# A recommendation tower on one core: ids loaded ahead of tables, and each pair's last gathered unit handled in two halves of its batches

## The chip, the cores and the metric

The kernel runs on one NeuronCore of a Trainium2 chip. The metric is the device time of one execution in microseconds (us), as a median over runs; lower is better.

## The reference

For each of 2048 batches, 26 rows of 128 numbers are looked up, one in each of 26 tables. The 27 vectors of a batch (the dense one and the 26 looked up) are multiplied with each other in pairs, and the 351 products, with the dense vector before and behind them, go through three dense layers.

```python
e = jnp.stack([tbl_0[ids[:, 0]], tbl_1[ids[:, 1]], ..., tbl_25[ids[:, 25]]], axis=1)
sd = jnp.einsum('bfd,bd->bf', e, r_dense_features)
ss = jnp.einsum('bfd,bgd->bfg', e, e)
pairs = ss[:, iu, ju]
z = jnp.concatenate([r_dense_features, sd, pairs], axis=1)
h = jnp.concatenate([z, r_dense_features], axis=1)
h = jnp.maximum(h @ W_top1 + b_top1, 0.0)
h = jnp.maximum(h @ W_top2 + b_top2, 0.0)
y = h @ W_top3
```

Everything is 32-bit floating point. The tables have 1000, 1250, 12500 or 125000 rows.

## The kernel before

The 2048 batches are cut into 8 chunks of 256, and two chunks make a pair: there are 4 pairs. All five engines have a program of their own, written out by hand, with semaphores between them. TensorE (PE) and ScalarE (ACT) both walk through the same list of steps for each pair, in the strings FIRST, SECOND, THIRD, LAST and TAIL; a step is a letter and a number, and each engine does its own part of the letters that concern it. The letters that matter here are these.

- `l`: one of the 12 (in later pairs 11) tables of 1000 rows is looked up on TensorE. The table lies in SBUF as two fp32r parts, `table_hi` and `table_lo`, and is multiplied with a one-hot matrix that VectorE (DVE) makes from the ids: 8 rows of the table for each of 125 partitions, in four parts, so 16 matmuls of 512 columns for a pair (L593). `c` is the copy of the result into `feat` by ScalarE (L434).
- `i` and `j`: ScalarE shifts the ids of one lookup for the one-hot comparison (L417). `s`: ScalarE makes `table_hi` of a table (L412). VectorE makes `table_lo` (L496), and then two comparisons for each of the four parts (L505). It does this for the tables in order, so that `make_part` of lookup 6 stands right behind its first `split_lo`, and waits for `ids_shifted`.
- `r` and `q`: a unit of gathered rows is turned. GpSimd (POOL) gathers the rows of the other 14 tables, two tables to a unit, with one indirect DMA for each table and each 128 batches: 4 a unit (L395), into a ring of 6 units. TensorE transposes the 4 blocks of 128x128 into one of two banks of `tr_ps` (L569), and ScalarE copies the bank into `feat` (L426). `q14` is the last unit of a pair, and belongs to its second chunk.
- `d` and `e`: the products of a chunk, in 8 steps of 32 matmuls (L611), `e` for the first chunk of a pair and `d` for the second. Step v covers batches 32v to 32v+31 of the chunk, so `d0` to `d3` read the first 128 batches and `d4` to `d7` the second. Each step's output is copied half by ScalarE (L441) and half by VectorE (L514).
- `k`, `o`, `m`: the dense layers of a chunk (L632, L641), for which the products go out to HBM and come back (L306, L319) through SyncE (SP).
- `f` and `g`: ScalarE copies the dense features of a chunk into `feat` (L421).

SyncE issues the loads in program order from L325 on: the first six tables with their ids, two more tables, the dense features of chunk 0, the row numbers (`idx`) of the gathers of pair 1, and then for u = 8 to 11 table u and ids u-2, and at last ids 10 and 11. A table is 1000x128 floats, 500 KB; the ids of one lookup are 128x512 of 16 bits, 128 KB; the dense features of a chunk are 128 KB, the `idx` of a pair 30 KB.

The wait at the head of the second chunk's products covers all the units of the pair:

```python
if v == 0:
    pe.wait_ge(transposed_out, unit_no(n // 2, UNITS if n % 2 else ALONE + has_odd(n // 2)))
```

Of the kernel before, what the change touches and what calls it, by code (L numbers as in the profile page):

```python
# [10 lines left out]
P = 128  # L11
# [9 lines left out]
CH = 256  # L21
# [47 lines left out]
SECOND = ("l0 l1 q12 l2 q13 l3 q14 d0 d1 d2 d3 d4 d5 d6 c2 d7 c3 r0 o0 c0 o1 c1 o2 r1 o3 r2 o4 i6 "  # L69
          "l4 c4 r3 i7 l5 c5 r4 i8 l6 c6 r5 l7 c7 i9 l8 c8 r6 i10 f l9 c9 r7 l10 c10 r8 "  # L70
          "j0 m0 g m1 e0 e1 e2 e3 r9 e4 e5 e6 e7 r10 m2 j1 m3 j2 r11 m4 j3 r12 j4 j5")
THIRD = ("l0 l1 q13 o0 q14 o1 d0 d1 d2 d3 d4 d5 d6 c0 d7 c1 r0 o2 o3 r1 o4 r2 "
         "l2 c2 r3 i6 l3 c3 i7 l4 c4 r4 i8 l5 c5 r5 l6 c6 i9 r6 l7 c7 i10 f l8 c8 r7 l9 c9 r8 l10 c10 r9 "
         "j0 m0 g m1 e0 e1 r10 e2 e3 e4 e5 e6 e7 r11 m2 j1 r12 m3 j2 j3 m4 r13 j4 j5")
LAST = ("l0 l1 q14 o0 o1 r0 d0 d1 d2 d3 d4 d5 d6 c0 d7 c1 r1 o2 o3 r2 o4 r3 "
        "l2 c2 l3 c3 r4 i6 l4 c4 r5 i7 l5 c5 i8 r6 l6 c6 i9 r7 f l7 c7 i10 l8 c8 r8 l9 c9 r9 g l10 c10 r10 "
        "m0 m1 e0 e1 e2 e3 r11 e4 e5 e6 e7 r12")
TAIL = "k2 q13 k3 q14 d0 d1 d2 d3 d4 d5 d6 d7 k4 o0 o1 o2 o3 o4 m0 m1 m2 m3 m4"
# [40 lines left out]
def dlrm_tower(nc, dense_t, dense_f, idx, ids_t, tables, w1, b1, w2, b2, w3, y):  # L119
# [6 lines left out]
    with ctx:  # L126
# [70 lines left out]
        onehot_read = sem("onehot_read")  # L197
        transposed = sem("transposed")
# [64 lines left out]
        def _(sp):  # L263
# [66 lines left out]
            for u in range(IDSLOTS, RAWS):  # L330
                load_table(u)
            load_dense(0)
            load_idx(1)
            for u in range(RAWS, NO + 1):
                load_table(u)
                load_ids(u - RAWS + IDSLOTS)
            for u in range(NO + 1 - RAWS + IDSLOTS, NO + 1):
                load_ids(u)
# [39 lines left out]
        @block.gpsimd  # L378
        def _(pool):
            nc.gpsimd.iota(row_i[:], [[1, 1]], base=0, channel_multiplier=-RPP)  # L380
            nc.gpsimd.iota(diag, [[1, P]], base=0, channel_multiplier=-1).then_inc(iotas_made, 1)

            for j, u in itertools.product(range(NPAIR), range(UNITS)):
                if u == ALONE and not has_odd(j):
                    continue
                i = unit_no(j, u)
                if u == 0:
                    pool.wait_ge(idx_loaded[j % 2], DMA * (j // 2 + 1))
                if i >= RING:
                    pool.wait_ge(transposed, i - RING + 1)  # L390
                for k in range(2):
                    f = ODD if u == ALONE else UNIT[u % (ALONE + 1)][k]
                    for t in range(TILES):
                        x = (2 * u + k) * TILES + t
                        nc.gpsimd.indirect_dma_start(  # L395
                            rows[:, i % RING, k, t, :], None, tables[f],
                            bass.IndirectOffsetOnAxis(ap=idx_sb[:, j % 2, x:x + 1], axis=0),
                        ).then_inc(rows_loaded[i % RING], DMA)
# [3 lines left out]
        def _(act):  # L402
# [20 lines left out]
            def transposed_to_feat(j, u):  # L423
                i = unit_no(j, u)
                act.wait_ge(transposed, i + 1)
                nc.scalar.activation(unit_view(u), tr_ps[:, i % 2], ACT.Copy).then_inc(transposed_out, 1)  # L426

# [27 lines left out]
            for j in range(NPAIR + 1):  # L455
                n = 2 * j
                for kind, x in steps(ORDER[j]):
# [12 lines left out]
                    if kind == "q":  # L470
                        transposed_to_feat(j - 1, x)
                    if kind == "f":
# [86 lines left out]
        def _(pe):  # L559
            def transposes(j, u):  # L560
                i = unit_no(j, u)
                pe.wait_ge(rows_loaded[i % RING], DMA * TILES * 2 * (i // RING + 1))
                if i == 0:
                    pe.wait_ge(ident_made, 1)
                if i >= 2:
                    pe.wait_ge(transposed_out, i - 1)
                for k in range(2):
                    for t in range(TILES):
                        last = nc.tensor.transpose(tr_ps[:, i % 2, k, t * P:(t + 1) * P], rows[:, i % RING, k, t, :],  # L569
                                                   ident[:])  # L570
# [28 lines left out]
            def dot_products(n, v):  # L599
                if v == 0:  # L600
                    pe.wait_ge(transposed_out, unit_no(n // 2, UNITS if n % 2 else ALONE + has_odd(n // 2)))
# [48 lines left out]
            for j in range(NPAIR + 1):  # L650
                n = 2 * j
                for kind, x in steps(ORDER[j]):
# [4 lines left out]
                    if kind == "q":  # L657
                        transposes(j - 1, x)
                    if kind == "d":
# [54 lines left out]
```

## Time and profile before

| | |
|---|---|
| median of 3 runs | 357.22 us (357.12 to 358.61) |
| the profiled execution, its own time | 358.96 us |
| its span, first to last instruction | 357.1 us |
| PE busy | 342.4 us, 96% |
| PE weight loads busy | 290.9 us, 81% |
| DVE busy | 207.0 us, 58% |
| ACT busy | 205.9 us, 58% |
| POOL busy | 239.0 us, 67% |
| mean granted clock of TensorE | 0.99 |

The span is measured between the first and the last instruction; the execution's own time has 1.9 us more around it. Busy time of PE counts matmuls from issue to their modelled end, so it says that PE nearly always has something in flight, and not that it runs at its peak. "PEclk" is the granted clock of TensorE as a share of full speed. A row of a timeline has start, duration, engine, line, operation, output and inputs with shapes, count, and in brackets the idle time of the engine just before it and what ended it.

### The profile page before, as it was taken

To read this page: it belongs to the slowest core of one execution; us is meant where nothing else is said; L and a number is where in the kernel's file an instruction comes from. 1 tells how busy PE (TensorE), PEld (TensorE's weight loads), DVE (VectorE), ACT (ScalarE), POOL (GpSimd) and SP (SyncE) were. 2 spreads that over 40 slices of the span, in tenths; PEclk is the share of its full clock that TensorE was granted. 3 is DMA by queue.
4 is the path that set the end of the run, shared out by engine and by line. 5 is a ranking of instruction groups with operands and counts; after the bars stand their busy time and mean duration, and the time that the engine had idled before them with its cause. 6 is when DMAs were issued, how large, how long until landed. Compare 5 with 4: busy or idle time off the path is not lost.

```text
span 357.1 us, 8384 instructions
## 1 busy us (share of the span) xinstructions
PE 342.4 (96%) x3412; PEld 290.9 (81%) x3412; DVE 207.0 (58%) x522; ACT 205.9 (58%) x268; POOL 239.0 (67%) x242
## 2 busy tenths in 40 slices
PE   8897899999899999999999999999999999998996
PEld 7575687788778888888988888898988888888885
DVE  4895899677504884716428784527327777235111
ACT  4674698762583657663565555772672675575111
POOL 5777777777777777777777777777777777700000
PEclk9999699999999999999999999999999999999999
DMA  7999829545246215263255224254246221223410
GB/s 192 237 232 229 216 54 285 146 104 148 56 116 197 54 45 156 56 147 107 59 131 168 63 61 143 54 120 137 54 101 185 73 62 50 53 58 98 97 40 2
DMA packets 46488, 40.94 MB, mean 115 GB/s; under 512 B 29059, under 2 KB 40443, under 8 KB 46451
## 3 DMA queue, kind: packets, MB, share of 16 engines
q1 hardware_dynamic: 38755, 24.81, 26.8%
q0 software_dynamic: 7552, 15.48, 17.2%
q8 instruction: 27, 0.44, 0.5%
q10 hardware_dynamic: 144, 0.13, 0.1%
q14 instruction: 10, 0.08, 0.1%
HBM read 34.64 MB, written 5.76 MB: 113 GB/s over the span
## 4 chain that ended last, share of the span: by engine, by line
PE 87%; DMA 7%; ACT 2%; DVE 2%; issue 1%; SPq 1%; ACTq 0%; DVEq 0%
PE oh_ps L593 39%; PE mlp_ps L632 16%; PE dot_ps L611 16%; PE mlp_ps L641 8%; PE tr_ps L569 7%; DMA ids_bc<-ids_t_dram 6%; PE mlp_ps L593 2%; DMA dots<-tbl_dram 2%; ACT feat L426 1%; DVE onehot L505 1%; ACT feat L434 0%; ACT ids_bc L417 0%; ACT table_hi L412 0%; DVE table_lo L496 0%; SPq L286 0%
## 5 line engine op out<-in xcount | busy, mean ns | idle before, releaser
L395 POOL DMA_INDIRECT rows<-tbl_dram,idx_sb x236 | 238.5, 1010 | 73.6 <-issue 70.7
L505 DVE TENSOR_SCALAR onehot<-ids_bc 125x512 fp32r<-125x512 int16 x360 | 142.9, 443 | 37.0 <-PE oh_ps L593 16.6
L593 PE MATMUL oh_ps<-onehot,table_hi 125*128 125x512 f32 x344 | 112.1, 408 | 5.4 <-DVE onehot L505 5.4
L593 PE MATMUL oh_ps<-onehot,table_lo 125*128 125x512 f32 x344 | 107.8, 395 | 0.0
L426 ACT ACTIVATE feat<-tr_ps 128x512 f32<-128x512 f32 x59 | 72.8, 1234 | 31.4 <-PE tr_ps L569 30.8
L434 ACT ACTIVATE feat<-oh_ps 128x512 f32<-128x512 f32 x43 | 52.4, 1219 | 55.2 <-PE oh_ps L593 54.5
L593 PEld LDWEIGHTS oh_ps<-onehot,table_hi 125*128 125x128 f32 x344 | 62.0, 192 | 20.4 <-issue 9.9
L593 PEld LDWEIGHTS oh_ps<-onehot,table_lo 125*128 125x128 f32 x344 | 65.5, 190 | 14.5
L611 PE MATMUL dot_ps<-feat 128*54 128x52 f32 x2048 | 57.9, 214 | 3.9 <-ACT feat L426 2.5
L611 PEld LDWEIGHTS dot_ps<-feat 128*54 128x54 f32 x2048 | 54.6, 130 | 8.6 <-issue 3.5
L514 DVE COPY dots<-dot_ps 54x416 f32<-54x416 f32 x56 | 33.3, 594 | 36.4 <-PE dot_ps L611 28.3
L632 PE MATMUL mlp_ps<-zt,w_sb 117*128 117x256 f32 x192 | 44.1, 380 | 0.8 <-ACT feat L434 0.8
L521 DVE TENSOR_TENSOR h<-mlp_ps,b_sb 128x256 f32<-128x256 f32 x16 | 6.8, 424 | 59.9 <-PE mlp_ps L641 59.9
L632 PEld LDWEIGHTS mlp_ps<-zt,w_sb 117*128 117x128 f32 x192 | 35.3, 190 | 5.3 <-issue 1.0
L441 ACT ACTIVATE dots<-dot_ps 54x416 f32<-54x416 f32 x56 | 28.9, 518 | 17.3 <-PE dot_ps L611 13.7
L569 PE MATMUL tr_ps<-ident,rows 128*128 128x128 f32 x236 | 36.0, 275 | 0.0
L417 ACT ACTIVATE ids_bc<-ids_bc,row_f 128x512 int16<-128x512 int16 x45 | 31.0, 702 | 6.5 <-DMA ids_bc<-ids_t_dram 6.5
L569 PEld LDWEIGHTS tr_ps<-ident,rows 128*128 128x128 f32 x236 | 28.5, 140 | 6.6
L448 ACT ACTIVATE h<-mlp_ps,b_sb 128x256 f32<-128x256 f32 x32 | 15.1, 471 | 25.9 <-PE mlp_ps L632 25.7
L641 PE MATMUL mlp_ps<-w_sb,h 128*128 128x256 f32 x128 | 29.0, 380 | 0.0
L641 PEld LDWEIGHTS mlp_ps<-w_sb,h 128*128 128x128 f32 x128 | 24.0, 190 | 3.1
L632 PE MATMUL mlp_ps<-feat,w_sb 117*128 117x256 f32 (+1 forms) x64 | 14.2, 379 | 0.0
(32 smaller groups left out, 98.3 us busy)
## 6 DMA issues: line engine op xcount, KB each, us to landing
ids_bc<-ids_t_dram SPq DMA_DIRECT2D x44, 128.0 KB, 3.4
dots_scratch<-dots SPq DMA_DIRECT2D x28, 175.5 KB
rows<-tbl_dram,idx_sb POOLq DMA_INDIRECT x236
dots<-tbl_dram SPq DMA_DIRECT2D x5, 480.0 KB
w_sb<-tbl_dram SPq DMA_DIRECT2D x3, 480.0 KB
zt<-dots_scratch SPq DMA_DIRECT2D x12, 117.0 KB
dense_sb<-dense_f_dram SPq DMA_DIRECT2D x8, 128.0 KB, 3.1
zt<-tbl_dram SPq DMA_DIRECT2D x2, 480.0 KB
```

The lines of the kernel that those rows point to most:

```text
L395: nc.gpsimd.indirect_dma_start(rows[:, i % RING, k, t, :], None, tables[f], bass.IndirectOffsetOnAxis(ap=idx_sb[:, j % 2, x:x + 1], axis=0 ...
L417: nc.scalar.activation(ids, ids, ACT.Identity, bias=row_f[:, 0:1]).then_inc(ids_shifted, 1)
L426: nc.scalar.activation(unit_view(u), tr_ps[:, i % 2], ACT.Copy).then_inc(transposed_out, 1)
L434: nc.scalar.activation(both, lookup_out(m).rearrange("p (c b) -> p c b", c=2), ACT.Copy).then_inc(looked_up_out, 1)
L441: nc.scalar.activation(*dot_copy(n, v, 0), ACT.Copy).then_inc(dots_out_act, 1)
L505: last = nc.vector.tensor_scalar(onehot_part(m, part)[:, c, :], ids_bc[0:TP, m % IDSLOTS, :], float(part * PROWS + c), None, ALU.is_equal)
L514: nc.vector.tensor_copy(*dot_copy(n, v, 1)).then_inc(dots_out_dve, 1)
L569: last = nc.tensor.transpose(tr_ps[:, i % 2, k, t * P:(t + 1) * P], rows[:, i % RING, k, t, :], ident[:])
L593: last = nc.tensor.matmul(lookup_out(m), table[0:TP, u, row * D:(row + 1) * D], onehot_part(m, part)[:, c, :], start=(table is table_hi an ...
L611: last = nc.tensor.matmul(dot_ps[dot_rows(t), v % 2, gi * PACK * NJ:(gi + 1) * PACK * NJ], batches.rearrange("p q f -> p (q f)"), batches[ ...
L632: last = nc.tensor.matmul(mlp_ps[:, x % 2, 0:CH], w1_sb[0:m, c, x * P:(x + 1) * P], z_of(n)[0:m, c, :], start=(c == 0), stop=(c == ZC))
L641: last = nc.tensor.matmul(mlp_ps[:, t, 0:N2], h1[:, c, t * P:(t + 1) * P], w2_sb[:, c, :], start=(c == 0), stop=(c == N1 // P - 1))
```

## The change

Two things are changed. SyncE issues the ids of lookup u-2 ahead of table u for u = 8 to 11, and issues the dense features of chunk 0 and the `idx` of pair 1 after all of these loads instead of before them. And the last unit of each pair is handled by halves of its batches: GpSimd gathers both tables' rows of the first 128 batches and then both of the second, each half with a semaphore of its own; step `q14` transposes and copies the first half only (2 transposes, a copy of 128x256), into columns 0 to 127 of one bank, and a new step `p` does the second, in the other bank. The products `d0` wait for the first half, and `d4` for the second.

```diff
--- before.py
+++ after.py
@@ -66,16 +66,16 @@
...
-SECOND = ("l0 l1 q12 l2 q13 l3 q14 d0 d1 d2 d3 d4 d5 d6 c2 d7 c3 r0 o0 c0 o1 c1 o2 r1 o3 r2 o4 i6 "
+SECOND = ("l0 l1 q12 l2 q13 l3 q14 d0 p d1 d2 d3 d4 d5 d6 c2 d7 c3 r0 o0 c0 o1 c1 o2 r1 o3 r2 o4 i6 "
...
-TAIL = "k2 q13 k3 q14 d0 d1 d2 d3 d4 d5 d6 d7 k4 o0 o1 o2 o3 o4 m0 m1 m2 m3 m4"
+TAIL = "k2 q13 k3 q14 d0 p d1 d2 d3 d4 d5 d6 d7 k4 o0 o1 o2 o3 o4 m0 m1 m2 m3 m4"
...
@@ -329,13 +333,13 @@
                 load_table(u)
             for u in range(IDSLOTS, RAWS):
                 load_table(u)
+            for u in range(RAWS, NO + 1):
+                load_ids(u - RAWS + IDSLOTS)
+                load_table(u)
+            for u in range(NO + 1 - RAWS + IDSLOTS, NO + 1):
+                load_ids(u)
             load_dense(0)
             load_idx(1)
-            for u in range(RAWS, NO + 1):
-                load_table(u)
-                load_ids(u - RAWS + IDSLOTS)
-            for u in range(NO + 1 - RAWS + IDSLOTS, NO + 1):
-                load_ids(u)
             load_dense(1)
             for u in range(3):
                 load_ids(looked(1) + u)
@@ -388,6 +392,14 @@
                     pool.wait_ge(idx_loaded[j % 2], DMA * (j // 2 + 1))
                 if i >= RING:
                     pool.wait_ge(transposed, i - RING + 1)
+                if u == UNITS - 1:
+                    for t, k in itertools.product(range(TILES), range(2)):
+                        x = (2 * u + k) * TILES + t
+                        nc.gpsimd.indirect_dma_start(
+                            rows[:, i % RING, k, t, :], None, tables[UNIT[ALONE - 1][k]],
+                            bass.IndirectOffsetOnAxis(ap=idx_sb[:, j % 2, x:x + 1], axis=0),
+                        ).then_inc(half_rows[t], DMA)
+                    continue
                 for k in range(2):
                     f = ODD if u == ALONE else UNIT[u % (ALONE + 1)][k]
                     for t in range(TILES):
@@ -422,8 +434,19 @@
 
             def transposed_to_feat(j, u):
                 i = unit_no(j, u)
+                if u == UNITS - 1:
+                    act.wait_ge(first_half_turned, j + 1)
+                    nc.scalar.activation(unit_view(u)[:, :, 0:P], tr_ps[:, i % 2, :, 0:P], ACT.Copy
+                                         ).then_inc(first_half_out, 1)
+                    return
                 act.wait_ge(transposed, i + 1)
                 nc.scalar.activation(unit_view(u), tr_ps[:, i % 2], ACT.Copy).then_inc(transposed_out, 1)
+
+            def second_half_to_feat(j):
+                i = unit_no(j, UNITS - 1)
+                act.wait_ge(transposed, i + 1)
+                nc.scalar.activation(unit_view(UNITS - 1)[:, :, P:CH], tr_ps[:, (i + 1) % 2, :, P:CH], ACT.Copy
+                                     ).then_inc(transposed_out, 1)
 
             def looked_up_to_feat(j, u):
                 m = looked(j) + u
...
@@ -557,17 +582,40 @@
 
         @block.tensor
         def _(pe):
+            def turn(j, u, bank, k, t):
+                i = unit_no(j, u)
+                return nc.tensor.transpose(tr_ps[:, bank, k, t * P:(t + 1) * P], rows[:, i % RING, k, t, :], ident[:])
+
             def transposes(j, u):
                 i = unit_no(j, u)
-                pe.wait_ge(rows_loaded[i % RING], DMA * TILES * 2 * (i // RING + 1))
+                if u == UNITS - 1:
+                    pe.wait_ge(half_rows[0], 2 * DMA * (j + 1))
+                else:
+
+                    ahead = sum(unit_no(h, UNITS - 1) % RING == i % RING for h in range(j))
+                    pe.wait_ge(rows_loaded[i % RING], DMA * TILES * 2 * (i // RING + 1 - ahead))
                 if i == 0:
                     pe.wait_ge(ident_made, 1)
                 if i >= 2:
-                    pe.wait_ge(transposed_out, i - 1)
+
+                    pe.wait_ge(transposed_out, i - (u > 0))
+                if u == UNITS - 1:
+                    for k in range(2):
+                        last = turn(j, u, i % 2, k, 0)
+                    last.then_inc(first_half_turned, 1)
+                    return
                 for k in range(2):
                     for t in range(TILES):
-                        last = nc.tensor.transpose(tr_ps[:, i % 2, k, t * P:(t + 1) * P], rows[:, i % RING, k, t, :],
-                                                   ident[:])
+                        last = turn(j, u, i % 2, k, t)
+                last.then_inc(transposed, 1)
+
+            def second_half(j):
+
+                i = unit_no(j, UNITS - 1)
+                pe.wait_ge(half_rows[1], 2 * DMA * (j + 1))
+                pe.wait_ge(transposed_out, i)
+                for k in range(2):
+                    last = turn(j, UNITS - 1, (i + 1) % 2, k, 1)
                 last.then_inc(transposed, 1)
 
             def lookup(j, u):
@@ -597,8 +645,14 @@
                     last.then_inc(onehot_read, 1)
 
             def dot_products(n, v):
+                if n % 2 and v == 0:
+                    pe.wait_ge(transposed_out, unit_no(n // 2, UNITS - 1))
+                    pe.wait_ge(first_half_out, n // 2 + 1)
+                if n % 2 and v == GUNITS // TILES:
+                    pe.wait_ge(transposed_out, unit_no(n // 2, UNITS))
+                if n % 2 == 0 and v == 0:
+                    pe.wait_ge(transposed_out, unit_no(n // 2, ALONE + has_odd(n // 2)))
                 if v == 0:
-                    pe.wait_ge(transposed_out, unit_no(n // 2, UNITS if n % 2 else ALONE + has_odd(n // 2)))
                     pe.wait_ge(looked_up_out, looked(n // 2 + 1))
                     pe.wait_ge(dense_out, n + 1)
                 if n or v >= 2:
...
```

Left out are the same new step `p` in THIRD (`q14 p o1 d0`) and LAST (`q14 p o0 o1 r0 d0`), the new semaphores, and the two lines by which TensorE and ScalarE do `p` for the pair before.

The loads that SyncE issues, from the last of the first eight tables on, in the kernel before (`dots`, `zt` and `w2_sb` hold raw tables here; `tbl_19` is table 8 in the text):

```order
L297 DMA w2_sb<-tbl_16_dram 5x1024
L278 DMA dense_sb<-dense_f_dram 128x256
L267 DMA idx_sb<-idx_dram 128x60
L296 DMA dots<-tbl_19_dram 120x1024 [waits lo_made]
L297 DMA dots<-tbl_19_dram 5x1024
L273 DMA ids_bc<-ids_t_dram 128x512 [waits onehot_made]
L296 DMA dots<-tbl_21_dram 120x1024 [waits lo_made]
```

The same place of the changed kernel:

```order
L301 DMA w2_sb<-tbl_16_dram 5x1024
L277 DMA ids_bc<-ids_t_dram 128x512 [waits onehot_made]
L300 DMA dots<-tbl_19_dram 120x1024 [waits lo_made]
L301 DMA dots<-tbl_19_dram 5x1024
L277 DMA ids_bc<-ids_t_dram 128x512 [waits onehot_made]
L300 DMA dots<-tbl_21_dram 120x1024 [waits lo_made]
```

The ids of lookup 6 stand right behind table 7: dense features, `idx` and table 8 are no longer ahead of them. The two small loads follow at the end of the row of loads:

```order
L300 DMA zt<-tbl_25_dram 120x1024 [waits lo_made]
L301 DMA zt<-tbl_25_dram 5x1024
L277 DMA ids_bc<-ids_t_dram 128x512 [waits onehot_made] x2
L282 DMA dense_sb<-dense_f_dram 128x256
L271 DMA idx_sb<-idx_dram 128x60
```

On TensorE, the last pair's last unit ahead of the last chunk's products (TAIL), in the kernel before:

```order
L632 MATMUL mlp_ps<-zt,w1_sb 128x256 x3
L569 MATMUL tr_ps<-ident,rows 128x128 [waits transposed_out,rows_loaded4]
L569 MATMUL tr_ps<-ident,rows 128x128 x3
L611 MATMUL dot_ps<-feat 54x52 [waits dots_out_act,dense_out,dots_out_dve,looked_up_out,transposed_out]
L611 MATMUL dot_ps<-feat 54x52 x15
L611 MATMUL dot_ps<-feat 54x52 [waits dots_out_dve,dots_out_act]
```

And in the changed kernel:

```order
L686 MATMUL mlp_ps<-zt,w1_sb 128x256 x3
L587 MATMUL tr_ps<-ident,rows 128x128 [waits transposed_out,half_rows0]
L587 MATMUL tr_ps<-ident,rows 128x128
L665 MATMUL dot_ps<-feat 54x52 [waits dense_out,dots_out_act,looked_up_out,dots_out_dve,first_half_out,transposed_out]
L665 MATMUL dot_ps<-feat 54x52 x15
L587 MATMUL tr_ps<-ident,rows 128x128 [waits transposed_out,half_rows1]
L587 MATMUL tr_ps<-ident,rows 128x128
L665 MATMUL dot_ps<-feat 54x52 [waits dots_out_dve,dots_out_act]
```

Two of the four transposes are moved behind `d0`, with a wait of their own for the second half of the rows.

## Rows read from the trace of the kernel before

**Rows 1.** The page: busy time of each engine.
```profile
PE 342.4 (96%) x3412; PEld 290.9 (81%) x3412; DVE 207.0 (58%) x522; ACT 205.9 (58%) x268; POOL 239.0 (67%) x242
```

**Rows 2.** Waits of PE: engine, line, waited for, us in total, times, longest.
```profile
PE oh_ps L593 <- DVE onehot L505: 5.4, 2, 4.1
PE dot_ps L611 <- ACT feat L426: 2.5, 2, 1.3
```

**Rows 3.** The chain that ended last, at the sixth ids: start, us, what.
```profile
14.79 20.59 DMA ids_bc<-ids_t_dram
...
35.41 0.73 ACT ids_bc L417
```

**Rows 4.** Timeline around PE's longest wait: DVE twice, then DVE and PE.
```profile
27.14 0.41 DVE L496 TENSOR_TENSOR table_lo<-w_sb,table_hi 125x256 fp32r<-125x256 f32 x1
...
31.27 0.41 DVE L496 TENSOR_TENSOR table_lo<-w_sb,table_hi 125x256 fp32r<-125x256 f32 x1
...
36.16 0.90 DVE L505 TENSOR_SCALAR onehot<-ids_bc 125x512 fp32r<-125x512 int16 x2 [4.48 <-ACT ids_bc L417]
...
37.20 1.19 PE L593 MATMUL oh_ps<-onehot,table_hi 125*128 125x512 f32 x2 [4.06 <-DVE onehot L505]
```

**Rows 5.** Windows: stretch, length, busy of PE, PEld, DVE, ACT, POOL, PEclk, DMA, GB/s.
```profile
33.14:37.20 4.06, 0.00 (x1) 0.03 (x1) 1.04 (x3) 1.79 (x3) 3.15 (x4) 0.87 1.01 234
37.20:43.43 6.23, 6.22 (x16) 4.88 (x17) 5.09 (x16) 3.69 (x4) 4.83 (x5) 0.53 0.92 226
43.98:47.50 3.52, 3.52 (x18) 2.93 (x17) 3.09 (x9) 3.52 (x4) 2.85 (x3) 1.00 0.27 75
```

**Rows 6.** Tile ids_bc on SP's queue: ids 5, 8 and 11 with landings.
```profile
L273 SPq DMA_DIRECT2D ids_bc<-ids_t_dram x1: 351/351/351, 8.5 to 8.5; - x1
DMA to landing us min/median/max: 12.3/12.3/12.3
...
L273 SPq DMA_DIRECT2D ids_bc<-ids_t_dram x1: 699/699/699, 24.2 to 24.2; - x1
DMA to landing us min/median/max: 18.4/18.4/18.4
...
L273 SPq DMA_DIRECT2D ids_bc<-ids_t_dram x1: 328/328/328, 31.4 to 31.4; - x1
DMA to landing us min/median/max: 14.5/14.5/14.5
```

**Rows 7.** Timeline, DVE: the one-hots of lookup 11's last part and the next six.
```profile
62.08 2.96 DVE L505 TENSOR_SCALAR onehot<-ids_bc 125x512 fp32r<-125x512 int16 x8
```

**Rows 8.** Timeline, ACT: the dense copy `f` and the table step `s10`.
```profile
51.45 0.83 ACT L421 ACTIVATE feat<-dense_sb 128x256 f32<-128x256 f32 x1
...
53.04 1.18 ACT L412 ACTIVATE table_hi<-dots 125x1024 fp32r<-125x1024 f32 x1
```

**Rows 9.** Timeline, PE: the products of chunk 1 after `q14` (SECOND).
```profile
91.42 7.46 PE L611 MATMUL dot_ps<-feat 128*54 128x52 f32 x256 [1.27 <-ACT feat L426]
```

**Rows 10.** Timeline of the tail: a dense copy, two gathers, `q14` and its copy.
```profile
302.68 0.77 ACT L421 ACTIVATE feat<-dense_sb 128x256 f32<-128x256 f32 x1
...
309.82 0.95 POOL L395 DMA_INDIRECT rows<-tbl_dram,idx_sb  x1 [0.30 <-issue]
...
312.32 0.94 POOL L395 DMA_INDIRECT rows<-tbl_dram,idx_sb  x1 [0.30 <-issue]
...
320.59 0.60 PE L569 MATMUL tr_ps<-ident,rows 128*128 128x128 f32 x4
...
321.23 1.18 ACT L426 ACTIVATE feat<-tr_ps 128x512 f32<-128x512 f32 x1
```

**Rows 11.** The chain: four transposes between products.
```profile
312.14 0.59 PE tr_ps L569 x4
```

**Rows 12.** Tile ids_bc on SP's queue, 52 to 54 us: landing of lone loads.
```profile
DMA to landing us min/median/max: 2.3/2.4/3.8
```

More of the change, by code:

```diff
@@ L68 @@
          "e4 e5 g j2 e6 e7 r11 j3 j4 j5")
-SECOND = ("l0 l1 q12 l2 q13 l3 q14 d0 d1 d2 d3 d4 d5 d6 c2 d7 c3 r0 o0 c0 o1 c1 o2 r1 o3 r2 o4 i6 "
+SECOND = ("l0 l1 q12 l2 q13 l3 q14 d0 p d1 d2 d3 d4 d5 d6 c2 d7 c3 r0 o0 c0 o1 c1 o2 r1 o3 r2 o4 i6 "
           "l4 c4 r3 i7 l5 c5 r4 i8 l6 c6 r5 l7 c7 i9 l8 c8 r6 i10 f l9 c9 r7 l10 c10 r8 "
           "j0 m0 g m1 e0 e1 e2 e3 r9 e4 e5 e6 e7 r10 m2 j1 m3 j2 r11 m4 j3 r12 j4 j5")
-THIRD = ("l0 l1 q13 o0 q14 o1 d0 d1 d2 d3 d4 d5 d6 c0 d7 c1 r0 o2 o3 r1 o4 r2 "
+THIRD = ("l0 l1 q13 o0 q14 p o1 d0 d1 d2 d3 d4 d5 d6 c0 d7 c1 r0 o2 o3 r1 o4 r2 "
          "l2 c2 r3 i6 l3 c3 i7 l4 c4 r4 i8 l5 c5 r5 l6 c6 i9 r6 l7 c7 i10 f l8 c8 r7 l9 c9 r8 l10 c10 r9 "
          "j0 m0 g m1 e0 e1 r10 e2 e3 e4 e5 e6 e7 r11 m2 j1 r12 m3 j2 j3 m4 r13 j4 j5")
-LAST = ("l0 l1 q14 o0 o1 r0 d0 d1 d2 d3 d4 d5 d6 c0 d7 c1 r1 o2 o3 r2 o4 r3 "
+LAST = ("l0 l1 q14 p o0 o1 r0 d0 d1 d2 d3 d4 d5 d6 c0 d7 c1 r1 o2 o3 r2 o4 r3 "
         "l2 c2 l3 c3 r4 i6 l4 c4 r5 i7 l5 c5 i8 r6 l6 c6 i9 r7 f l7 c7 i10 l8 c8 r8 l9 c9 r9 g l10 c10 r10 "
         "m0 m1 e0 e1 e2 e3 r11 e4 e5 e6 e7 r12")
-TAIL = "k2 q13 k3 q14 d0 d1 d2 d3 d4 d5 d6 d7 k4 o0 o1 o2 o3 o4 m0 m1 m2 m3 m4"
+TAIL = "k2 q13 k3 q14 d0 p d1 d2 d3 d4 d5 d6 d7 k4 o0 o1 o2 o3 o4 m0 m1 m2 m3 m4"
 ORDER = [FIRST, SECOND, THIRD, LAST, TAIL]
@@ L197, in dlrm_tower @@
         onehot_read = sem("onehot_read")
+        half_rows = [sem(f"half_rows{t}") for t in range(TILES)]
+        first_half_turned = sem("first_half_turned")
+        first_half_out = sem("first_half_out")
         transposed = sem("transposed")
@@ L471, in _ @@
                         transposed_to_feat(j - 1, x)
+                    if kind == "p":
+                        second_half_to_feat(j - 1)
                     if kind == "f":
@@ L658, in _ @@
                         transposes(j - 1, x)
+                    if kind == "p":
+                        second_half(j - 1)
                     if kind == "d":
```

## The prediction

> **What bounds the kernel now.** I read the page first: PE is busy for 96% of the span and the other engines for 58 to 67% [rows 1], so time is lost only where PE stands still or runs slowly. The waits of PE name both places: 5.4 us for one-hots, of which one wait is 4.1 us, and 2.5 us, in two waits, for ScalarE's copy of a unit ahead of the products [rows 2]. A third loss is not a wait at all: the windows show TensorE's clock.
>
> The long wait, followed back. The chain says that the ids of lookup 6 were issued at 14.79 and landed 20.59 us later, at 35.38, that ScalarE then shifted them [rows 3], and that VectorE, idle for 4.48 us, began the one-hots at 36.16; PE, idle for 4.06 us, started lookup 6 at 37.20 [rows 4]. The table part that VectorE makes just before these one-hots was there at 31.27 + 0.41 = 31.68 [rows 4], so it was the ids alone that were missing. They were late because of what SyncE had put ahead of them: in issue order dense features, `idx` and table 8, and those behind tables 5 to 7.
>
> The clock. In the stretch in which PE idles, the granted clock falls (0.87 on average), and in the whole of lookup 6 behind it, it is 0.53, so near the lower level of 1.2 GHz; in lookup 7 it is 1.00 again [rows 5]. Lookup 6 with its 16 matmuls takes 6.23 us, lookup 7 takes 3.52 in the stretch shown [rows 5].
>
> **The ids moved ahead.** From the landing of ids 5 (8.5 + 12.3 = 20.8) [rows 6] to that of ids 6 (35.4) the queue moved tables 5 to 8, dense features, `idx` and ids 6, 2000 + 128 + 30 + 128 = 2286 KB in 14.6 us, 157 KB a us. From ids 6 to ids 8 (24.2 + 18.4 = 42.6) [rows 6] it moved two tables and two ids, 1256 KB in 7.2 us, 174 KB a us. The change takes table 8, dense features and `idx`, 658 KB, out from ahead of ids 6: 4.2 us by the first rate, 3.8 by the second. I take 4.2, since it is the rate of that very stretch; ids 6 then land at 31.2, and VectorE starts 0.78 later as before, at 31.98, 0.3 us after its table part is ready. PE ends the transposes ahead of lookup 6 at 33.14 and needs the one-hots about 1.04 us after VectorE begins (36.16 to 37.20), so at 33.02: no wait.
>
> From there VectorE sets the pace. Its first table parts of lookups 5 and 6 stand 31.27 - 27.14 = 4.13 us apart [rows 4]. From the first one-hots of lookup 6 to the last part of lookup 11 are 5.75 lookups, 23.7 us. Before, they took 62.08 - 36.16 = 25.9 [rows 4, 7]: 2.2 us more, lost while PE at half clock held the one-hot buffers. Now the last part starts at 31.98 + 23.7 = 55.7 instead of 62.08, **6.35 us earlier** (4.2 of wait and 2.15 of slow clock). Lookups 7, 8 and 9 need their ids at 36.1, 40.2 and 44.4. Counting the bytes ahead of each, ids 7 now stand where ids 6 stood, less dense features and `idx`, plus ids 7: 35.2 + 0.8 for the shift, 36.0. Ids 8 come one table and one load of ids later (628 KB, 4.0 us), shifted at 40.0, ids 9 at 44.0. All are just in time, none with more than 0.4 us in hand.
>
> **The 2.15 us hang on what made the clock fall.** The rows show one fall, behind PE's longest wait: 0.13 x 4.06 + 0.47 x 6.23 = 3.5 us of missing clock [rows 5] is 1% of the span, all that its mean of 0.99 lacks, so PE's shorter waits (1.3 us and less [rows 2]) left it alone. If the clock fell for the idle time, no idle time means no fall, and the result is my sum, 351.4; if it fell for another cause, 2.15 us of the gain are gone, 353.6. The Trainium skill (TensorE: Matmul & The Clock Gate, Part 1: The HAM clock gate) says that the throttled state is the default and that activity releases it. By that rule the sum stays whole, and the trace agrees: 0.53 behind the idle stretch, 1.00 after one lookup.
>
> **The two loads moved behind.** The dense features of chunk 0 now come last. The bytes in the queue are the same in all, so they land about when ids 11 did, 31.4 + 14.5 = 45.9 [rows 6]. ScalarE copies them at 51.45 before and goes on to table 10's high part at 53.04 to 54.22 [rows 8]. Shifted by 6.35, the copy is wanted at 45.1 and the high part is done at 47.87, where VectorE wants it at 31.6 + 4 x 4.13 = 48.1. So ScalarE waits 0.8 to 1.0 us, 0.2 of it is slack, and **0.7 us** passes through VectorE to PE. It would be nothing if the loads drain faster, and 1.2 if the small load lands later still. `idx` of pair 1 is wanted by GpSimd only after 56 gathers of pair 0 at its pitch of 1.25 us or more (309.82 to 312.32 are two) [rows 10], so after 70 us: no cost. No load other than these three kinds changes place on SyncE.
>
> **The unit in halves.** Nothing is added to GpSimd's 236 gathers, which are only reordered. At the first boundary (SECOND) PE waits 1.27 us for the copy [rows 9]. Two transposes less ahead of the copy are 0.3 us (half of 0.60), and a copy of 128x256 takes 0.77 where 128x512 takes 1.18 [rows 10]: `d0` starts 0.7 earlier. Step `p` then costs PE two transposes between products; four cost 0.59 [rows 11], so 0.3, and I add 0.1 for the second switch. Net -0.3. ScalarE's second copy of 0.77 lies between its copies for `d0` and `d1`, where PE is not waiting for it: two banks are free before `d2`. In TAIL the copy starts at 321.23, after PE's transposes were done, because ScalarE is busy with a relu until then, so only 0.4 of copy is saved, and `p` costs 0.4: nothing. In THIRD and LAST the copy was hidden before by a layer step; there `p` costs 0.1 each for its wait and switch. Bounds of this part: -1.2 (two boundaries at 0.7, with transposes for nothing) to +0.9 (four times 0.4 less 0.7). Sum **-0.1**.
>
> **Sum.** -6.35 + 0.7 - 0.1 = **-5.8 us**. The profiled execution took 358.96 with a span of 357.1, so it would take 353.2 with a span of 351.3; it stood 1.7 above the median, and from the median, 357.22, I forecast 351.4.
>
> Does the gain live to the end? PE has work queued everywhere behind, and what could hold it is the gathers, since GpSimd never waits for PE and so doesn't move. Its last gather starts at 312.32 and ends at 313.26; `q14` comes at 320.59 [rows 10]. Lone loads land 2.3 to 3.8 us after issue [rows 12], so I let the rows land by 315.7 at best, by 317.1 at worst. With 5.8 us less, `q14` comes at 314.8 and needs only the first half, whose second gather starts at 309.82 and which lands by 314.6 at worst. `p` comes behind relu, copy and `d0`, at about 317.2. It is ready. Whole, the unit would have made PE wait 0.9 us or more, so here the halves guard what the ids win, and that is their use in the tail.
>
> **Rivals.**
> - *The wait moves to the next ids.* The queue stays full until 43 us, and ids 7 and 8 have 0.1 us in hand. If the queue is slower by a tenth, PE stands still for 1 to 2 us in pieces, and perhaps at a lower clock: 352.6 to 354.4. For it: the small margins. Against it: both rates come from this stretch. 0.14.
> - *The clock falls all the same*: 353.6, as above. 0.07.
> - *Issue order does not decide landing*, so the first part does nothing; with the halves alone, 357.1. The Trainium skill (DMA: Bandwidth & Descriptors, Queues, rings and completion order) says that descriptors are consumed in ring order, but that a later one may finish its write first. The landings of ids 6, 8 and 11 (35.4, 42.6, 45.9) follow the order and the bytes. 0.05.
> - *The last half of rows is late*: a gather that takes 4.8 us to land makes PE wait 1 us in `p`: 352.4. 0.05.
> - *Slower.* The dense copy `f` stands in ScalarE's order ahead of lookup 8's copy and of table 10, and ScalarE cannot pass it. From a landing of the dense features at 51.1 (45.1 + 0.2 + 5.8) on, the change costs more than it brings; with PE idle that long the clock would fall again, another 2.2 us, so it decides from about 49. At 52.5 the result is 361. For it: the loads are now last in the queue, behind two loads of ids that wait for one-hots. Against it: those waits are over at 31.4, the issue of ids 11 [rows 6]. 0.04.
>
> **Numbers.** The forecast has the rest, 0.65. A measurement of this kernel can tell about 0.5%, 1.8 us, from no change, so faster is below 355.4. The low end takes the full 6.35 with no wait for dense features and 0.9 at the boundaries, 350.0; the high end holds the cases of moved wait, kept slow clock and late half, 354.4. Left out are the third and fifth rival and the edges. Faster 0.90: all but those two. Same 0.06, slower 0.04.
>
> **What would show it.** In the new profile ids 6 land near 31 and PE goes from lookup 5 to 6 with under 1 us between; PEclk stays at 1.00 from 30 to 50 us; ScalarE's copy of dense features waits for a DMA at about 45 us; the products of chunk 0 begin near 60 instead of 65.5; PE's wait ahead of chunk 1's products is about 0.6 instead of 1.27; the last `p` waits for nothing and the last gather still starts near 312. The prediction is wrong if PEclk falls again, if ids 7 or 8 hold PE, or if PE waits in `p`.

## The result, and the profile after

The changed kernel takes **353.26 us** in the median of four runs (352.86 to 353.53), the kernel before took 357.59 beside it (357.12 to 358.61). The ratio is 0.9874, 95% interval 0.9849 to 0.99: faster, by 1.3%. The profiled execution took 353.4 with a span of 351.6, where before's had 358.96 and 357.1. One thing has to be known of the experiments: in two of their three sets every kernel, the one before included, took 466 to 488 us at a mean granted clock near 0.9, and the ratios, which are taken from the shorter executions of each kernel alone, can lie above 1 there while the medians of all lie below, so they decide little.

The page of the changed kernel, against [rows 1]:

```profile
PE 340.6 (97%) x3412; PEld 288.8 (82%) x3412; DVE 206.8 (59%) x522; ACT 205.7 (58%) x272; POOL 239.0 (68%) x242
...
PEclk9999999999999999999999999999999999999999
```

The first line is busy time by engine, the second TensorE's granted clock in 40 equal slices of the span, in tenths (9 is 90% or more). The waits of PE in the changed kernel, against [rows 2] (engine, tile and line, waited for: us in total, times, longest):

```profile
PE dot_ps L665 <- issue: 3.0, 4, 1.0
...
PE tr_ps L587 <- DMA rows<-tbl_dram,idx_sb: 1.3, 1, 1.3
...
PE oh_ps L641 <- DVE onehot L530: 0.8, 1, 0.8
```

Of 5.4 us for one-hots 0.8 is left, that of the first lookup. ScalarE's copy of a unit is no longer what the profile names at the end of a wait ahead of products; the gaps that are left there it calls "issue", which is time for which it shows no releaser. A new line has come in: 1.3 us for gathered rows, ahead of transposes.

The timeline of the changed kernel at the old long wait, ScalarE's rows first, then PE's, against [rows 3, 4]:

```profile
29.96 0.70 ACT L429 ACTIVATE ids_bc<-ids_bc,row_f 128x512 int16<-128x512 int16 x1
...
34.09 0.71 ACT L429 ACTIVATE ids_bc<-ids_bc,row_f 128x512 int16<-128x512 int16 x1
```
```profile
31.92 0.60 PE L587 MATMUL tr_ps<-ident,rows 128*128 128x128 f32 x4
32.28 0.70 PE L641 MATMUL oh_ps<-onehot,table_hi 125*128 125x512 f32 x2
...
37.48 0.66 PE L587 MATMUL tr_ps<-ident,rows 128*128 128x128 f32 x4 [1.28 <-DMA rows<-tbl_dram,idx_sb]
```

ScalarE shifts ids 6 at 29.96 (35.41 before) and ids 7 at 34.09 without waiting for either, and PE goes from the transposes into lookup 6 with no gap. The ids were issued at 11.5 and landed 18.4 us later, at 29.9. PE now waits at 37.48 instead, for rows.

The windows of 30 to 50 us (length, busy of PE, PEld, DVE, ACT, POOL, PEclk, DMA share, GB/s), of the changed kernel and then of the kernel before:

```profile
30.00:50.00 20.00, 18.62 (x89) 14.55 (x88) 18.95 (x55) 17.48 (x20) 15.43 (x16) 1.00 0.76 191
```
```profile
30.00:50.00 20.00, 15.94 (x64) 12.72 (x63) 13.90 (x40) 12.06 (x14) 15.43 (x16) 0.83 0.73 176
```

The clock no longer falls, and PE gets 89 matmuls done in this stretch instead of 64. GpSimd's column is the same in both: 16 gathers, since it waits for nobody here.

The chain that ended last, in the changed kernel, a little later:

```profile
33.28 1.04 POOL rows L407
34.32 0.31 issue
34.62 7.22 DMA rows<-tbl_dram,idx_sb
41.85 0.04 issue
41.89 0.66 PE tr_ps L587 x4
```

These rows took 7.22 us from the gather to the landing, where the page's median over all 236 gathers is 3.2. They came just in time for PE, the ones before them 1.3 us late.

Two of the four boundaries with a unit in halves, those at which PE had waited for the copy (SECOND and TAIL), in the changed kernel, against [rows 9, 10]:

```profile
83.80 0.38 PE L587 MATMUL tr_ps<-ident,rows 128*128 128x128 f32 x2
85.00 1.01 PE L665 MATMUL dot_ps<-feat 128*54 128x52 f32 x32 [0.81 <-issue]
85.93 0.44 PE L587 MATMUL tr_ps<-ident,rows 128*128 128x128 f32 x2
86.30 6.68 PE L665 MATMUL dot_ps<-feat 128*54 128x52 f32 x224
...
314.73 0.38 PE L587 MATMUL tr_ps<-ident,rows 128*128 128x128 f32 x2
316.07 1.01 PE L665 MATMUL dot_ps<-feat 128*54 128x52 f32 x32 [0.96 <-issue]
317.01 0.44 PE L587 MATMUL tr_ps<-ident,rows 128*128 128x128 f32 x2
317.38 3.00 PE L665 MATMUL dot_ps<-feat 128*54 128x52 f32 x104
320.77 3.40 PE L665 MATMUL dot_ps<-feat 128*54 128x52 f32 x120 [0.39 <-issue]
```

`q14`, `d0` and `p` stand as the change puts them, and `p` waits for nothing in either place. Read against the kernel before, PE is 5.74 us ahead at the first products (65.54 to 59.80), 6.42 at the products of chunk 1 (91.42 to 85.00), 5.86 at `q14` of the tail (320.59 to 314.73) and 5.47 at the last layer steps behind the products (329.57 to 324.10).

### The profile page after: what moved, and what is told of

Its sections match the earlier page's. It is cut to its first block, busy times and chain, and to the rows that moved or that the text cites. A ratio compares the mean times of both kernels' runs of the same rounds, so it can differ in the third digit from the quotient of the medians.

```text
span 351.6 us, 8396 instructions
## 1 busy us (share of the span) xinstructions
PE 340.6 (97%) x3412; PEld 288.8 (82%) x3412; DVE 206.8 (59%) x522; ACT 205.7 (58%) x272; POOL 239.0 (68%) x242
## 4 chain that ended last, share of the span: by engine, by line
PE 85%; POOL 7%; issue 3%; DMA 3%; ACT 1%; DVE 0%; ACTq 0%; DVEq 0%
PE oh_ps L641 36%; PE dot_ps L665 16%; PE mlp_ps L686 16%; PE mlp_ps L695 8%; PE tr_ps L587 7%; POOL rows L407 7%; PE mlp_ps L641 2%; DMA rows<-tbl_dram,idx_sb 2%; DMA idx_sb<-idx_dram 1%; ACT feat L443 0%; ACT feat L457 0%; DVE h L549 0%; ACT ids_bc L429 0%; DVE h L546 0%; ACT dots L464 0%
## 5 line engine op out<-in xcount | busy, mean ns | idle before, releaser
L641 PE MATMUL oh_ps<-onehot,table_hi 125*128 125x512 f32 x344 | 110.7, 403 | 0.8 <-DVE onehot L530 0.8
L641 PE MATMUL oh_ps<-onehot,table_lo 125*128 125x512 f32 x344 | 106.5, 391 | 0.0
L443 ACT ACTIVATE feat<-tr_ps 128x512 f32<-128x512 f32 x55 | 68.2, 1241 | 23.1 <-PE tr_ps L587 22.5
L641 PEld LDWEIGHTS oh_ps<-onehot,table_lo 125*128 125x128 f32 x344 | 64.6, 188 | 14.1
L641 PEld LDWEIGHTS oh_ps<-onehot,table_hi 125*128 125x128 f32 x344 | 60.8, 189 | 15.4 <-issue 6.0
```

The costliest lines, as they stand in the source:

```text
L641: last = nc.tensor.matmul(lookup_out(m), table[0:TP, u, row * D:(row + 1) * D], onehot_part(m, part)[:, c, :], start=(table is table_hi an ...
```

## The experiments

The theory was that the load order brings nearly all of the gain, as a wait and a slow clock that are both gone, and that the halves bring next to nothing by themselves and guard the gain in the tail. The rivals: the halves bring a good part of it; the clock's fall has another cause than idle time; the late rows cost what the ids win.

**A first set, of the parts.** Four kernels ran side by side. The kernel before, unchanged:

> The kernel before, unchanged. The changed kernel is 5.5 us shorter in the profiled spans, but 4.3 us in the medians. Theory: how long the clock stays at half level after the long wait differs from one execution to the next, so spans lie between about 355 and 357.1 and go with the mean clock (0.990 at 357.1, up to 0.995 at 355). Rival: the 1.2 us are time outside the span; then spans are 357 every time and the clock 0.990.

The load order alone (its edit stands with the second set):

> Only the order of SyncE's loads is changed; the last unit stays whole. Theory (the load order brings nearly all): span 351.6, within 0.5 us of the changed kernel; the products after q14 begin 5.7 us earlier at both exposed boundaries, and in the tail PE waits 0.3 us for the last rows (last gather issued at 312.3, landing 2.7 us). Rival (the halves carry part of it): PE waits over 1 us for the last rows, span 352.6 or more.

The halves alone:

> Only the last unit of each pair is done in halves; the loads are as before. Theory: what the earlier start of d0 saves (0.7 and 0.6 us at two boundaries) is given back by step p between products (0.4 to 0.9 each): span 357.0 to 357.6, no difference. Rival (the halves gain at the exposed boundaries, as forecast for SECOND): 356.5 or less.

And the change with the two small loads kept in front of ids 6:

```diff
+            load_dense(0)
+            load_idx(1)
             for u in range(RAWS, NO + 1):
                 load_ids(u - RAWS + IDSLOTS)
                 load_table(u)
             for u in range(NO + 1 - RAWS + IDSLOTS, NO + 1):
                 load_ids(u)
-            load_dense(0)
-            load_idx(1)
```

> The changed kernel, with dense features and idx ahead of ids 6 as before; only the ids stay ahead of the tables. Ids 6 then land 0.9 us later, near 30.9. Theory (behind the ids it is the landing of gathered rows that holds PE, at 37.5 us, whatever the one-hots do): span within 0.3 us of 351.6. Rival (VectorE's pace from ids 6 on sets the stage, as in my prediction): 0.7 us longer, 352.3.

The kernel before took 481.88 beside these (470.15 to 488.43, 23 runs). In the order above the medians were 478.25, 478.97, 478.49 and 479.52, the ratios 0.9992 (0.9878 to 1.0107), 0.999 (0.9906 to 1.0074), 1.0144 (1.0052 to 1.0236) and 1.0141 (1.0052 to 1.0231). The waits of PE in the unchanged kernel of this set say why that settles nothing:

```profile
PE dot_ps L611 <- issue: 33.3, 55, 1.2
PE oh_ps L593 <- DVE onehot L505: 19.9, 14, 4.1
PE oh_ps L593 <- issue: 18.6, 11, 4.6
```

These three rows hold 72 us of waits, spread over the whole span, and one-hots alone 20 us where [rows 2] have 5.4. A kernel with such gaps on every engine has other ends of waits than ours. Nor do the two ratios of 1.014 say that halves cost anything: they stand beside medians that are lower than the 481.88 of the kernel before.

**A second set, at the usual speed.** The kernel before took 356.97 (354.75 to 359.43, 25 runs). Against this median the changed kernel's 353.26 would be 0.9896, so its gain is better told as 1.0 to 1.3%: the four executions beside it had a median of 357.59.

The load order alone, on the kernel before:

```diff
-            load_dense(0)
-            load_idx(1)
             for u in range(RAWS, NO + 1):
-                load_table(u)
                 load_ids(u - RAWS + IDSLOTS)
+                load_table(u)
             for u in range(NO + 1 - RAWS + IDSLOTS, NO + 1):
                 load_ids(u)
+            load_dense(0)
+            load_idx(1)
```

> Only the order of SyncE's loads is changed; the last unit stays whole. Theory (the load order brings nearly all): span 351.6, within 0.5 us of the changed kernel; the products after q14 begin 5.7 us earlier at both exposed boundaries, and in the tail PE waits about 0.3 us for the last rows (last gather issued at 312.3, landing 2.7 us). Rival (the halves carry part of it): PE waits over 1 us for the last rows, span 352.6 or more.

Measured: 357.08 (355.26 to 358.25, ten runs), ratio 0.9998, interval 0.9965 to 1.0031. **The load order alone brings nothing that can be measured.** Its profile shows that it works where it should and loses the gain at the end. The timeline of PE in the tail:

```profile
311.04 0.66 PE L569 MATMUL tr_ps<-ident,rows 128*128 128x128 f32 x4
...
313.26 0.60 PE L569 MATMUL tr_ps<-ident,rows 128*128 128x128 f32 x4
313.70 1.90 PE L632 MATMUL mlp_ps<-zt,w_sb 117*128 117x256 f32 x8
317.14 0.66 PE L569 MATMUL tr_ps<-ident,rows 128*128 128x128 f32 x4 [1.55 <-DMA rows<-tbl_dram,idx_sb]
319.07 9.70 PE L611 MATMUL dot_ps<-feat 128*54 128x52 f32 x256 [1.27 <-ACT feat L426]
```

The chain at its last gather:

```profile
312.17 0.95 POOL rows L395
313.11 0.30 issue
313.42 3.68 DMA rows<-tbl_dram,idx_sb
```

And the windows there, of this kernel (the columns are those of the windows above):

```profile
310.00:315.00 5.00, 5.00 (x68) 4.52 (x63) 1.19 (x2) 3.75 (x5) 3.45 (x4) 1.00 0.38 89
315.00:320.00 5.00, 2.18 (x27) 1.54 (x27) 0.00 (x0) 1.74 (x3) 0.00 (x0) 0.81 0.62 146
320.00:325.00 5.00, 5.00 (x114) 5.00 (x112) 1.78 (x3) 1.53 (x3) 0.00 (x0) 0.51 0.25 75
325.00:330.00 5.00, 5.00 (x142) 4.65 (x139) 2.97 (x5) 2.56 (x5) 0.00 (x0) 1.00 0.02 7
```

PE comes to its first products at 60.47, 5.07 us ahead of before, and is still 5.16 ahead at `q13` (318.42 to 313.26). Then it reaches the last unit before its rows do: the chain has the last gather at 313.42 and 3.68 us to the landing. It waits 1.55 us, transposes for 0.67 us, waits 1.27 us for the whole unit's copy, and in the second of those waits the clock falls to the lower level (1.00 up to 317.80, 0.62 on average from there to 319.07, 0.50 behind it): the last 256 products take 9.70 us where they took 7.18 at 322.46 in the kernel before. By the steps behind them (329.57 to 328.70) 0.87 of the 5.16 us is left. In this profile the fall is not at the ids any more (PEclk is 1.00 from 30 to 50 us), it is at the end.

The size of that first wait has scatter in it. The last gather started at 313.42 here and at 312.32 in the kernel before. From there the same 3.68 us would have left PE a wait of about 0.4 us (an estimate: 316.0 less 315.6, where PE stopped). But two kernels with halves had a last gather nearly as late, at 313.08 (the halves alone, below) and 313.34 (units later, below), and PE waited for no rows in their tails, with `q14` at 315.11 and 314.80. In the profiles, then, the halves do guard the tail.

The halves alone, that is the change with the load order of the kernel before:

> Only the last unit of each pair is done in halves; the loads are as before. Theory: what the earlier start of d0 saves (0.7 and 0.6 us at two boundaries) is given back by step p between products (0.4 to 0.9 each): span 357.0 to 357.6 if the clock falls for as long as before, no difference. Rival (the halves gain at the exposed boundaries, as forecast for SECOND): 356.5 or less.

Measured: 355.72 (353.65 to 361.1, ten runs), ratio 0.9961, interval 0.9918 to 1.0003: a gain of 1.3 us at the edge of what can be told. Its profiled execution had a span of 351.8, as short as the changed kernel's, although its ids are loaded in the old order. Rows of that execution, ScalarE and PE at lookup 6:

```profile
32.08 0.72 ACT L429 ACTIVATE ids_bc<-ids_bc,row_f 128x512 int16<-128x512 int16 x1 [1.79 <-DMA ids_bc<-ids_t_dram]
```
```profile
33.78 0.70 PE L641 MATMUL oh_ps<-onehot,table_hi 125*128 125x512 f32 x2 [1.03 <-DVE onehot L530]
```

Here ScalarE, which waited for ids 6, took them up at 32.08 where it was 35.41 in [rows 3], 3.3 us earlier with the same loads in the same order, PE waited 1.03 us instead of 4.06, and the clock stayed at 1.00. The windows of 20 to 30 us, of the kernel before and then of this one, show where the 3.3 us come from:

```profile
20.00:30.00 10.00, 10.00 (x52) 8.07 (x51) 10.00 (x30) 8.88 (x10) 7.87 (x8) 1.00 1.01 234
```
```profile
20.00:30.00 10.00, 10.00 (x51) 8.11 (x50) 10.00 (x30) 9.23 (x10) 7.87 (x8) 1.00 1.00 258
```

With the DMA engines full in both (shares 1.01 and 1.00), they moved 234 GB/s in one execution and 258 in the other. Why is not shown. So **the loss that the change removes has no fixed size**. The other runs say the same: the 25 executions of the kernel before have spans from 352.9 to 357.6, eight at a mean clock of 1.00 or 0.999 (352.9 to 354.3), the others at 0.99 to 0.995 (353.2 to 357.6). Where the clock did not fall, the load order alone has little left to win: three of its executions have a clock of 1.00, with spans of 352.9 to 353.4. The changed kernel's four are at 351.1 to 351.7.

PE kept busy while it waits, to part the wait from the clock:

```diff
+                        if j == 0 and x == 6:
+                            for i in range(FILL):
+                                last = nc.tensor.transpose(mlp_ps[:, i % 2, 0:P], ident[:], ident[:])
+                            last.then_inc(warmed, 1)
                         lookup(j, x)
```

with FILL = 34, on the kernel before (left out is that the first lookup to write into `mlp_ps` waits for the filling too).

> The kernel before, with 34 more transposes of the identity on TensorE ahead of lookup 6, about 3.7 us of work that nobody reads, so that PE is not idle while it waits for ids 6. Theory (the clock fell because PE was idle): PEclk 1.00 throughout, lookup 6 still starts at 37.2, and the span is 2.0 us shorter than before, 355.1. Rival (the clock falls for another cause, such as the full DMA queue): the clock falls at 36 us as before and the span stays at 357.1.

Measured: 357.22 (356.19 to 359.79, ten runs), ratio 1.0027, interval 0.9996 to 1.0058. The windows of its profile:

```profile
30.00:50.00 20.00, 20.00 (x115) 17.12 (x114) 16.97 (x50) 15.41 (x18) 15.43 (x16) 1.00 0.69 171
```

and PE's rows at lookup 6:

```profile
33.43 3.88 PE L657 MATMUL mlp_ps<-ident 128*128 128x128 f32 x34
37.06 0.70 PE L594 MATMUL oh_ps<-onehot,table_hi 125*128 125x512 f32 x2
```

With PE never idle the clock stays at 1.00 in a run whose ids came late (shifted at 34.07), and seven of its ten runs had a mean clock of 1.00 or 0.999, against eight of the 25 of the kernel before. Both speak for idle time as the cause, though this profile is a milder case than [rows 4]: its one-hots began at 34.83, so without filling PE would have waited about 2.3 us and not 4.06 (an estimate, with the 1.04 us from VectorE's start to PE's in [rows 4]). Even in the wait of [rows 4] the clock was still at 1.00 from 35 to 36 us and fell behind it, so this profile alone doesn't show that the filling is what kept the clock. The rival, a full DMA queue, is out: in the changed kernel the clock stayed at 1.00 over 30 to 37 us at a DMA share of 1.00, and in the tail of the load order alone it was at 0.51 with a share of 0.25. Lookup 6 starts where it did (37.06, before 37.20) and the first products stand 25.61 us behind it instead of 28.34 (62.67 and 65.54): at full clock the way from there is 2.7 us shorter. The Trainium skill (TensorE: Matmul & The Clock Gate, Part 1: The HAM clock gate) has activity release the throttled state, and this run agrees with its 1.00. But nothing is won in the median. The fill holds PE for 3.6 us (33.43 to 37.06) in every execution, also where the ids land early, and three of the ten runs still had a mean clock of 0.995; where it fell in those is not known.

The units of rows turned one lookup later, in the changed kernel, against the new wait at 37.48 (the line below is cut to the steps that move):

```diff
-         "r4 l7 c7 s9 i9 r5 f l8 c8 s10 i10 r6 l9 c9 s11 i11 l10 c10 r8 ..."
+         "l7 c7 s9 i9 r4 f l8 c8 s10 i10 r5 l9 c9 s11 i11 r6 l10 c10 r8 ..."
```

> The changed kernel, with r4, r5 and r6 of the first pair each one lookup later in the list (r6 takes the free place ahead of lookup 10). Theory (gathered rows that land 7 to 8 us after issue hold PE for 1.3 us and 0.5 us ahead of lookups 7 and 8): those waits go and the span is 1.0 to 1.5 us shorter, 350.3. Rival (VectorE's pace of 4.13 us a lookup takes the place at once): waits for one-hots of the same size appear and the span stays within 0.4 of 351.6.

Measured: 353.19 (352.75 to 353.68, four runs), ratio 0.9896, interval 0.9854 to 0.9938. The windows:

```profile
30.00:50.00 20.00, 19.96 (x92) 14.79 (x91) 19.45 (x58) 17.03 (x20) 15.43 (x16) 1.00 0.78 199
```

The wait for rows is gone, PE is busy for 19.96 of the 20 us instead of 18.62. From the first matmul of lookup 0 to the first products it takes 47.54 us (11.97 to 59.51), the changed kernel 48.47 (11.33 to 59.80). Of these 0.9 us the whole run keeps too little to see: the profiled execution began its first lookup 0.64 later, with a wait of 1.51 for its first one-hots where the changed kernel had 0.80, and its span is 351.4 against 351.6. So late rows cost 0.9 us in their stage, and the start of the program moves by as much from one profile to the next (first lookups at 11.33 to 12.35 in six).

**A third set, on the tail.** It fell again on a chip where the kernel before took 479.89 (468.23 to 487.41, 31 runs). The changed kernel once more:

> The changed kernel once more, beside many executions of the kernel before. Theory: the kernel before varies with the landing of ids 6 (spans 352.9 to 357.6, mean clock 1.00, 0.995 or 0.99), and the changed one does not, because neither the ids nor the last rows leave PE idle for long: spans 351.0 to 352, clock 1.00 in every execution. Rival (the changed kernel was lucky in its four): spans over 353 and clocks of 0.995 appear in some of them.

The first half turned one step earlier, in both places where the products of chunk 1 and of the last chunk follow it at once:

```diff
-SECOND = ("l0 l1 q12 l2 q13 l3 q14 d0 p d1 ..."
+SECOND = ("l0 l1 q12 l2 q13 q14 l3 d0 p d1 ..."
...
-TAIL = "k2 q13 k3 q14 d0 p ..."
+TAIL = "k2 q13 q14 k3 d0 p ..."
```

> The changed kernel with the first half's step q14 one step earlier at the two boundaries where its copy is exposed: q13 q14 l3 d0 p in SECOND and q13 q14 k3 d0 p in TAIL. Theory (PE's waits of 0.8 and 1.0 us ahead of d0 are for ScalarE's copy of the first half, and lookup 3 or the layer step can cover it): both waits go, span 349.9. Rival (the rows of the first half have not landed that early, or ScalarE's order delays the copy behind other work): one wait stays or moves ahead of q14, span 350.8 or more.

The load order alone, with twelve transposes that nobody reads ahead of the last unit's and ten behind them:

> Only the load order is changed, as in f1, and in the tail TensorE does 12 transposes that nobody reads ahead of q14 and 10 more behind it, in the 1.55 us and 1.27 us in which it stood idle. Theory (with the last unit whole, these two waits close together bring the clock down, and the last products then take 9.7 us instead of 7.2): PEclk stays at 1.00 in the tail, products 7.2 us, span 353.7 and 2.5 us below f1's profile. Rival (the products were slow for another cause): 9.7 us again, 356.2.

The change, with only the last pair's unit in halves:

> The changed load order, and halves for the last pair's last unit only; the other three pairs turn and copy it whole. Theory (only in the tail does the unit come so late that its halves matter; at SECOND they save 0.7 us ahead of the products and give 0.5 back): within 0.3 us of the changed kernel, span 351.4 to 351.9. Rival (the halves earn at SECOND too): 352.0 or more.

Medians and ratios, in this order: 477.71, 1.0077 (1.0005 to 1.0149); 473.0, 0.9899 (0.9815 to 0.9984); 482.32, 0.9947 (0.9844 to 1.005); 479.92, 1.004 (0.9974 to 1.0106). The changed kernel itself, which is 1.0 to 1.3% faster where the chip runs at its usual speed, shows no gain here, so none of the others can be judged from this set. The second, from six executions, is the only one whose interval lies below 1; it is a hint that an earlier first half helps, no more. Open stay: whether filling would keep the clock in the tail, whether halves at the first three boundaries do anything, and what the order of the two small loads is worth by itself.

## Why the prediction was right, and where not

The side was right and the range held the time. The forecast gave the profiled execution 353.2 us and a span of 351.3; it took 353.4 and 351.6. From the median it forecast 351.4, and 353.26 came. So its sum fits one execution to 0.3 us and misses the median by 1.9. Step by step:

- **Ids ahead: right.** They landed at 29.9 (forecast 31.2; the loads went through faster in this execution, 246 GB/s over 20 to 30 us where before had 234), no wait was left ahead of lookup 6, PEclk stayed at 1.00. The step of 6.35 us can be read in the run with the units later, where nothing else holds PE: from the start of lookup 0 to the first products 53.70 us before (11.84 to 65.54), 47.54 there, **6.16 less**.
- **Dense features late, +0.7: wrong, it was 0.** They landed at 31.2 + 12.6 = 43.8, not at 45.9, and ScalarE copied them at 45.40 without waiting. The term took the landing over from ids 11 of [rows 6]; those landed earlier too, at 30.8 + 12.7 = 43.5. The margin is thin: in the load order alone they landed at 32.1 + 13.1 = 45.2, just as ScalarE took them up (45.20).
- **Left out: rows that land late.** "What could hold it is the gathers" was asked of the tail alone, so the sum has no term for them at 30 to 50 us. PE ran 5 us earlier, GpSimd did not, and with the queue full rows took 7.2 us to land: 0.9 us in this stage (the changed kernel's 48.47 against 47.54). That the two errors nearly cancel is luck: the stage was forecast at -5.65 and measured, from lookup 0 on, at 48.47 - 53.70 = -5.23. Another 0.5 came from an earlier start of lookup 0 (11.33 instead of 11.84), which is scatter.
- **The halves, -0.1: right in its parts.** At the first boundary the way to `d0` is 0.68 shorter (65.54 to 91.42 is 25.88, 59.80 to 85.00 is 25.20; forecast 0.7), and the products with `p` take 0.52 more (7.39 us up to the next transposes at 98.81, now 7.91; forecast 0.4). From there to `q14` of the tail nothing changes, 221.78 and 221.82, where 0.2 was forecast. In the tail `q14` to `d0` is 0.53 shorter, and the products take 8.03 instead of 7.11, but 0.39 of that is a gap called "issue" that the two other kernels with halves don't have; both take 7.62. Without that gap the halves come to -0.1, with it to +0.3. (The lower bound of this part, -1.2, should be -1.4 by its own terms, twice 0.7, and the low end of the range counts only 0.9 of it.)
- **"From the median, 357.22, I forecast 351.4": this step failed.** The 5.8 us are the size that the loss had in the profiled execution, which was 1.7 slower than the median. The loss is just what differs between executions: ids 6 landed at 35.4, 34.05 and about 32.05 in three profiles with the old order. The times of before spread over 4.7 us in 25 executions, those of the changed kernel over 0.7 in four, and with the units later over 0.9 in four. What is left once the loss is gone looks steady, so the forecast should have been the profiled execution's own time less the sum, 353.2. The range held because its high end, 354.4, had room for other losses, not because this one was seen. The scatter could not be seen in one profile, but its 358.96 beside a lowest run of 357.12 was a sign.
- **"The halves guard what the ids win": right in kind, far too small in size.** It was priced at 0.9 us of wait. The load order alone showed 1.55 us of wait, 1.1 of them by a later last gather, and then 2.5 us of clock (9.70 against 7.18), and its median gives back all of the gain. The prediction priced only the wait for rows and not what a second wait, 1.27 us for the copy, does to the clock right behind it.

Of the rivals, ids 7 and 8 held nobody, the clock did not fall, issue order did decide, the last `p` had its rows, and the dense copy was on time. But the first of these was hardly tested: it asked for a slower queue, and the queue was faster. Why the DMA engines move a tenth more in one execution than in another, and so land the ids 3 us apart, is not explained here; nor is it shown that the waits and the clock of the profiled execution are those of the executions behind the median of the load order alone, whose mean clocks were 1.00 (three), 0.995 (four) and 0.99 (three).

## What to carry to other kernels

A gain early in a program has to be followed to every later point where PE meets something that keeps its own time, here the gathers: first while the queue is full, then at the last one. Two edits of which each alone is worth nothing or little (0.9998 and 0.9961) can be worth over 1% together, so price the second with the first already made. And where the loss that an edit removes varies from execution to execution, take the time that is left from one execution, don't take the loss of one from the median of all.

## What the runs showed of the hardware

- Rows of a gather landed 7.2 us after the gather while SyncE's loads kept the DMA engines full (share 1.00 in the changed kernel's 30 to 37 us, 233 GB/s), against a median of 3.2 over the program and 3.68 for the last one of the load order alone.
- Two waits of 1.55 and 1.27 us with 0.67 us of transposes between them were followed by a granted clock of 0.51 over 320 to 325 us; the same 1.27 us alone, in [rows 9] and in the tail of the kernel before (1.00 in each five us from 310 to 325), was not.
- The same loads in the same order landed 3.3 us apart in two executions, which moved 234 and 258 GB/s over 20 to 30 us at a DMA share of 1.01 and 1.00.
- The same program took 357 us on one chip and about 480 on two others, with gaps of up to 4.6 us called "issue" ahead of matmuls and a mean granted clock of 0.88 to 0.91.
